# Zeroing the later keys with GpSimd instead of masking them with TensorE in the causal steps of two attention stages

## The chip, the cores and the metric

The kernel is one program on one core of a Trainium2 chip. The metric is the device time of the whole program in microseconds (us). Five engines work side by side, each through its own list of instructions in order, and they wait for each other on semaphores: PE is TensorE (PEld is its weight load), DVE is VectorE, ACT is ScalarE, POOL is GpSimd, SP is SyncE, which issues most DMAs.

## The reference

A decoder of four layers is computed for eight batches of 256 tokens of width 256. The change lies in two stages of layer 1, in which every batch has a causal softmax over its own 256 tokens with 16 heads of 16:

```python
# L1_attn, first half of the block (then LayerNorm, feed-forward, LayerNorm)
mask = (tq[:, :, None] >= tk[:, None, :]) & (tk[:, None, :] >= 0)
sim = jnp.where(mask[None], jnp.einsum('bnwd,bnkd->bnwk', qw, bk), -1000000000.0)
out = jnp.einsum('bnwk,bnkd->bnwd', jax.nn.softmax(sim, axis=-1), bv)

# L1_xattn, first of its two attentions (the second looks at 77 context rows, no mask)
scores = jnp.where(jnp.tril(...), q @ k * scale, finfo.min)
out = softmax(scores) @ v
```

Windows are 128 wide and each sees itself and the one before it, so for 256 tokens this is plain causal attention.

## The kernel before

Both stages are pipelined over steps p. In L1_attn there is one step for each batch (p = 0 to 7) and two more to drain. In L1_xattn there are sixteen: causal steps (called a) and context steps (b), in the order a0 a1 a2 b0 a3 b1 ... a7 b5 b6 b7. In step p the order of instructions of each engine is written out by hand; in it `now` is the batch of this step, `last` and `older` the two before, `soon` the next. Nothing is reordered later: an engine that waits stops everything behind the wait.

The attention of a causal batch goes like this.

- `pair_scores_tensor`, rounds 0 to 2: scores with queries in the partitions, 4 banks of PSUM (2048 columns). The later keys are masked by four matmuls of an identity with a mask of large negative numbers (`hide_later`, line 517). `pair_tops_vector` (line 569) takes each query's maximum, one VectorE reduction a round, and the next round reuses the banks, so TensorE and VectorE take turns here.
- `split_tops_vector` (lines 578 to 584) splits the maxima into three bf16 parts, `turn_tops_tensor` (592) transposes them, `turn_tops_scalar` (599) copies them out as `mT`.
- Turned scores, rounds 0 to 2, with keys in the partitions: `turned_first_tensor` and `turned_scores_tensor`. In each round four `hide_later` matmuls write the mask `keyC` to the banks, `turned_products` (line 621) adds the scores, and `turned_maxima` (line 630) subtracts the maxima. `turned_probs_scalar` (line 675) takes the exponential of 2048 columns into SBUF (`prob1` for round 0, `prob` for rounds 1 and 2) and raises `prob`; the next round may then overwrite the banks.
- `pair_outputs_tensor` c = 0 and 1 (lines 689 and 694) multiplies the probabilities of heads 8c to 8c+7 with the values; `pair_raw_scalar` (702) copies the results; `pair_back_tensor` (711) and `mean_vector` (721, 723) turn and divide them.

The tail of an L1_attn step on TensorE is, before: `turned_scores` 1; `own_v` of `soon` (line 416); `turned_scores` 2; outputs c = 0 of `now`; a wait for `kv` of `soon`, which VectorE raises in `own_v_vector` (line 796) and which frees PSUM bank 3; the queries of `soon` into bank 3; the second feed-forward product of `older`. The next step begins with scores 0 of the next batch, outputs c = 1 of this one, and the transposes of `older`. VectorE in the same step: three reductions, the split, `own_k_vector` (759), `mean_vector` of `last`, in steps 3 to 6 the second LayerNorm of batch p-3 (`outer_norm_vector`: statistics 2048 and 2052, a run of ten short dependent instructions at 2054 and 277 to 281, then 2057 and 2061), `own_v_vector` (796), the first LayerNorm of `last` (`inner_norm_vector`, from line 2087 on), `turned_z_vector` (830), `outer_sum_vector` (2096).

The tail of a causal L1_xattn step on TensorE: `turned_scores` 2, in some steps a product of the fp8 stage, outputs c = 0 of `now`; then the next step with its scores 0 (which wait for the last exponential) and outputs c = 1.

GpSimd does one bias addition for each batch in L1_xattn (line 864), and in L1_attn that and `x1b` (line 2266).

Of the kernel before, what the change touches and what calls it, by code (L numbers as in the profile page):

```python
# [18 lines left out]
ALU = mybir.AluOpType  # L19
# [3 lines left out]
P = 128  # L23
B, SEQ, D = 8, 256, 256
# [72 lines left out]
def places(fields):  # L97

    at, out = 0, {}
    for name, n in fields:  # L100
# [3 lines left out]

COMMON = ("done", "dve_step", "z", "zT_ps", "zT", "qkv_ps", "q", "kv", "s_ps", "s_sb", "prob", "probT_ps", "probT_a",
          "probT_v", "o_ps", "raw", "back_ps", "o", "oT_ps", "oT", "out_ps", "ctx")


# [70 lines left out]
def cut(ap, **sizes):  # L181
    (name, n), = sizes.items()
    return ap.rearrange(f"p ({name} f) -> p {name} f", **{name: n})
# [80 lines left out]
def mask_of(k, name):  # L264
    at, n = k.maskpos[name]
    return k.masks[:, at:at + n]
# [213 lines left out]
def narrow_signals(a):  # L480
    per = dict(kv_ps=1, kv=1, q_ps=1, q=1, s_ps=a.rounds, top=a.rounds, part=4, mT_ps=1, mT=1, t_ps=a.rounds,
               prob=a.rounds, o_ps=2, raw=2, back_ps=1, rec=1, o=1)
    if a.causal:
        per.update(z=1, zT_ps=1, zT=1, k_ps=1, k=1)
    return {a.p + name: n for name, n in per.items()}


# [28 lines left out]
def hide_later(k, out, mask):  # L516
    k.nc.tensor.matmul(out, k.identb[:, :], mask, start=True, stop=False, skip_group_check=True)  # L517
# [84 lines left out]
def turned_places(u, r):  # L602

    every, later, first, second, own = slice(0, SEQ), slice(P, SEQ), slice(0, P), slice(P, SEQ), slice(0, CTX)
    if not u.a.causal:
        return [(2 * r + ab, every, own, ab * SEQ) for ab in (0, 1)]
    if r == 0:
        return [(j, later, second, j * P) for j in range(4)]
    return [(2 * r - 2 + ab, every, first, ab * SEQ) for ab in (0, 1)]
# [26 lines left out]
def turned_first_tensor(k, pe, s, u, b, at=0):  # L636

    after(pe, s, u, "top", u.a.rounds)
    causal, places = u.a.causal, turned_places(u, 0)
    if causal:  # L640
        for i in range(4):
            hide_later(k, k.ps[:, HI + i, :], mask_of(k, "keyC"))
    else:
        turned_products(k, s, u, places[0], True, False)
    turn_tops_tensor(k, pe, s, u, b, at)
    for place in places if causal else places[1:]:
        turned_products(k, s, u, place, False, False)
    after(pe, s, u, "mT")
    for place in places:
        ins = turned_maxima(k, s, u, place, False, True)  # L650
    ins.then_inc(*s.sig.up(u.a.p + "t_ps"))


def turned_scores_tensor(k, pe, s, u, r):

    after(pe, s, u, "prob", r)
    if u.a.causal:
        for i in range(4):
            hide_later(k, cut(k.ps[:, HI + i, :], slot=4)[:, 0::2, :], mask_of(k, "keyC")[:, 0:2 * P])
    for place in turned_places(u, r):  # L660
        turned_maxima(k, s, u, place, not u.a.causal, False)
        ins = turned_products(k, s, u, place, False, True)
    ins.then_inc(*s.sig.up(u.a.p + "t_ps"))

# [14 lines left out]
def pair_outputs_tensor(k, pe, s, u, before, c):  # L679

    v, nk = s.v[u.at], u.a.nk
    after(pe, s, u, "prob", u.a.rounds - 1 + c)
    if u.a.causal:
        after(pe, s, u, "kv")
    after(pe, s, before, "o")
    for j in (2 * c, 2 * c + 1):
        at = j % 2 * SEQ
        for i in range(4):
            ins = k.nc.tensor.matmul(k.ps[PAD * i:PAD * i + u.a.vw, LO + c, at:at + SEQ], v[0:nk, 0, 4 * j + i, :],  # L689
                                     s.prob[0:nk, i, j * SEQ:(j + 1) * SEQ], start=True, stop=not u.a.causal,  # L690
                                     skip_group_check=True)
        if u.a.causal:
            for i in range(4):
                ins = k.nc.tensor.matmul(k.ps[PAD * i:PAD * i + VW, LO + c, at + P:at + SEQ], v[:, 1, 4 * j + i, :],
                                         s.prob1[:, i, j * P:(j + 1) * P], start=False, stop=True,
                                         skip_group_check=True)
    ins.then_inc(*s.sig.up(u.a.p + "o_ps"))


def pair_raw_scalar(k, act, s, u, c):  # L700
# [729 lines left out]

def L1_xattn_gpsimd(k, pool, s):
    enter(k, pool, s.sig)
    for n in range(B):
        bias_gpsimd(k, pool, s, n, "z", "bo2")


CHUNKS = 10
# [693 lines left out]
def L1_attn_tensor(k, pe, s):  # L2131
    pe.wait_ge(*s.behind.sig.at("f_out", 0, B - 1, 1))
    one = s.ahead
    own = one.steps[0]
    for p in range(B + 2):
        now, last, older, soon, _ = neighbours(s.steps, p)
        if now:
            pair_scores_tensor(k, pe, s, now, last, 0)
        if last:
            pair_outputs_tensor(k, pe, s, last, older, 1)  # L2140
        if older:
            after(pe, s, older, "x1")
            if p >= 3:
                after(pe, s, s.steps[p - 3], "sum")
            turn_tensor(k, s.x1[older.n % 2], k.ps[:, 2, :]).then_inc(*s.sig.up("x1T_ps"))
        if now:
            pair_scores_tensor(k, pe, s, now, last, 1)
        if soon:
            turned_z_tensor(k, pe, s, soon, 3)
        if p == B:  # L2150
            turned_z_tensor(k, pe, one, own, HI)
        if older:
            ff_up_tensor(k, pe, s, older, 0, 2)
        if p == B + 1:
            own_v_tensor(k, pe, one, own, HI + 3)
        if now:
            pair_scores_tensor(k, pe, s, now, last, 2)
        if last:
            pair_back_tensor(k, pe, s, last)
        if soon:  # L2160
            own_k_tensor(k, pe, s, soon, 3)
        if now:
            if older:
                after(pe, s, older, "f", 1)
            turned_first_tensor(k, pe, s, now, 2)
        if p == B:
            pe.wait_ge(*k.loaded["L1_xattn"])
            own_k_tensor(k, pe, one, own, HI + 1)
        if older:
            ff_up_tensor(k, pe, s, older, 1, 2)  # L2170
        if p == B:
            query_tensor(k, one, own, one.zT, HI + 2)
        if now:
            turned_scores_tensor(k, pe, s, now, 1)
        if soon:
            own_v_tensor(k, pe, s, soon, 3)
        if now:
            turned_scores_tensor(k, pe, s, now, 2)
            pair_outputs_tensor(k, pe, s, now, last, 0)
        if soon:  # L2180
            after(pe, s, soon, "kv")
            query_tensor(k, s, soon, s.zT, 3)
        if older:
            after(pe, s, older, "f", 2)
            token_out_tensor(k, s, s.f, w_of(k, s.stage, "ff2", FF // P), 2, FF // P).then_inc(*s.sig.up("out_ps"))


def L1_attn_scalar(k, act, s):
    one = s.ahead
    own = one.steps[0]  # L2190
    for p in range(B + 2):
        now, last, older, soon, _ = neighbours(s.steps, p)
        if last:
            pair_raw_scalar(k, act, s, last, 1)
        if older:
            after(act, s, older, "x1T_ps")
            k.nc.scalar.activation(flat(s.x1T), k.ps[:, 2, :], ACT.Copy).then_inc(*s.sig.up("x1T"))
        if soon:
            turned_z_scalar(k, act, s, soon, 3)
        if p == B:  # L2200
            turned_z_scalar(k, act, one, own, HI)
        if older:
            ff_up_scalar(k, act, s, older, 0, 2)
        if now:
            turn_tops_scalar(k, act, s, now, 2)
            turned_probs_scalar(k, act, s, now, 0)
        if older:
            ff_up_scalar(k, act, s, older, 1, 2)
        if p == B:
            query_scalar(k, act, one, own, HI + 2)  # L2210
        if now:
            turned_probs_scalar(k, act, s, now, 1)
            turned_probs_scalar(k, act, s, now, 2)
            pair_raw_scalar(k, act, s, now, 0)
        if soon:
            query_scalar(k, act, s, soon, 3)


def L1_attn_vector(k, dve, s):
# [36 lines left out]
            outer_sum_vector(k, dve, s, older, 2)  # L2256


def L1_attn_gpsimd(k, pool, s):
    enter(k, pool, s.sig)  # L2260
    for u in s.steps:
        bias_gpsimd(k, pool, s, u.n, "z", "ln2_b")
        pool.wait_ge(*s.sig.at("x1", 0, u.n, 1))
        if u.n >= 2:
            pool.wait_ge(*s.sig.at("sum", 0, u.n - 2, 1))
        k.nc.gpsimd.tensor_tensor(s.x1b[u.n % 2], s.x1[u.n % 2],
                                  spread_of(k, s.stage, "ff2b").unsqueeze(1).broadcast_to([P, 2, D]), ALU.add)\
            .then_inc(*s.sig.up("x1b"))

# [3040 lines left out]
```

## Time and profile before

| | us |
|---|---|
| three timed runs | 3136.51, 3142.32, 3145.74 |
| their median | 3142.32 |
| the profiled execution, from first to last instruction | 3146.4 |
| TensorE busy in it | 2939.7 (93%) |
| VectorE busy | 1864.8 (59%) |
| ScalarE busy | 1253.5 (40%) |
| GpSimd busy | 435.9 (14%) |

A row of the timeline has the start of a run of equal instructions in us from the start of the span, its length, engine, line, operation, operands with shapes, and how many there are. In brackets stands how long the engine had been idle and which engine and line ended the wait. The first mask matmul of the changed stages starts at 1136.6 and the last at 1681.1; L1_attn fills about 1136 to 1400, L1_xattn 1400 to 1700.

### The profile page before, as it was taken

How to read it: one execution, taken by the hardware profiler on the slowest of the kernel's cores; microseconds unless marked ns; L12 is line 12 of the kernel's file. 1: busy time of each engine (PE TensorE's matmuls, PEld its weight loads, DVE VectorE, ACT ScalarE, POOL GpSimd, SP SyncE). 2: the span in 40 equal slices, each digit the busy share in tenths (PEclk: the TensorE clock that was granted, in tenths of full speed). 3: DMA queues.
4: the chain of work that ended last, by engine and by line, in shares of the span. 5: the costliest groups of instructions: out<-in, count | busy, mean ns of one | idle time of the engine just before them, and what ended most of it. 6: DMA issues, size and time to landing. Idle time of an engine off the chain costs nothing.

```text
span 3146.4 us, 52294 instructions
## 1 busy us (share of the span) xinstructions
PE 2939.7 (93%) x20677; PEld 1953.5 (62%) x20677; DVE 1864.8 (59%) x6449; ACT 1253.5 (40%) x1946; POOL 435.9 (14%) x458
## 2 busy tenths in 40 slices
PE   7999999998989889988998999899999999998998
PEld 4666666875555556655665566566666766766653
DVE  5534433599999636775777898574244344434455
ACT  2222221335656433323444678544323333323443
POOL 0010010114433221000000356300000000000000
PEclk9999999988999999999999899899999999998999
DMA  3000000010000100000000111100000000000000
GB/s 130 1 1 0 1 1 1 1 53 1 2 1 2 34 32 1 1 1 6 1 2 1 25 39 28 41 2 27 1 1 0 1 0 1 1 1 9 2 1 27
DMA packets 22028, 37.75 MB, mean 12 GB/s; under 512 B 2132, under 2 KB 19733, under 8 KB 20760
## 3 DMA queue, kind: packets, MB, share of 16 engines
q1 hardware_dynamic: 20968, 34.02, 3.2%
q8 instruction: 163, 2.67, 0.3%
q14 instruction: 81, 0.66, 0.1%
q10 hardware_dynamic: 816, 0.39, 0.1%
HBM read 26.81 MB, written 2.10 MB: 9 GB/s over the span
## 4 chain that ended last, share of the span: by engine, by line
PE 76%; DVE 17%; ACT 4%; issue 2%; DMA 0%; ACTq 0%; DVEq 0%; SPq 0%; POOL 0%; POOLq 0%
PE ps L416 44%; DVE arena L569 3%; PE ps L621 2%; PE ps L689 2%; PE ps L3098 2%; PE ps L3117 2%; ACT arena L675 2%; PE ps L1633 2%; PE ps L517 2%; PE ps L2353 2%; PE ps L2399 2%; DVE arena L1967 2%; PE ps L730 2%; PE ps L711 1%; PE ps L2971 1%
## 5 line engine op out<-in xcount | busy, mean ns | idle before, releaser
L416 PE MATMUL ps<-weights,arena 128*128 128x256 f32 (+4 forms) x2480 | 694.3, 429 | 41.3 <-DVE arena L1848 22.5
L416 PEld LDWEIGHTS ps<-weights,arena 128*128 128x128 f32 (+1 forms) x2480 | 459.5, 195 | 210.8 <-issue 92.9
L416 PE MATMUL ps<-arena,weights 128*128 128x256 f32 (+4 forms) x1726 | 558.9, 472 | 14.0 <-DMA weights<-in_w_L_attn 6.1
L416 PEld LDWEIGHTS ps<-arena,weights 128*128 128x128 f32 (+1 forms) x1726 | 315.1, 191 | 217.0 <-issue 156.5
L416 PE MATMUL ps<-arena 128*128 128x256 f32 (+4 forms) x1618 | 425.8, 416 | 6.8 <-ACT arena L4816 1.5
L416 PEld LDWEIGHTS ps<-arena 128*128 128x128 f32 (+2 forms) x1618 | 297.9, 188 | 115.4 <-issue 74.3
L569 DVE TENSOR_REDUCE arena<-ps 128x16 f32<-128x1232 f32 (+2 forms) x96 | 179.1, 1866 | 151.0 <-PE ps L547 51.8
L675 ACT ACTIVATE arena<-ps 77x2048 f32<-77x2048 f32 (+1 forms) x112 | 210.0, 1875 | 123.9 <-PE ps L621 61.8
L1967 DVE MATCH_REPLACE8 arena<-arena 128x77 f32<-128x77 f32 x1024 | 214.7, 228 | 0.0
L864 POOL TENSOR_TENSOR x<-x,weights 128x512 f32<-128x512 f32 x32 | 43.8, 1370 | 1194.9 <-DVE arena L830 1147.2
L2366 ACT ACTIVATE arena<-ps 128x1536 f32<-128x1536 f32 x128 | 185.5, 1451 | 51.4 <-PE ps L2355 44.6
L2384 POOL TENSOR_SCALAR_AFFINE_SELECT arena<-arena 128x512 f32<-128x512 f32 x128 | 147.5, 1154 | 217.6 <-ACT arena L2366 217.1
L1960 DVE MAX8 arena<-arena 128x8 f32<-128x77 f32 x1024 | 154.1, 229 | 0.2 <-DVE rstd L281 0.2
L4199 DVE COPY arena<-ps 128x1024 f32<-128x1024 f32 x16 | 19.6, 1225 | 203.8 <-PE ps L416 203.8
L4061 ACT ACTIVATE arena<-ps 128x512 f32<-128x512 f32 x128 | 76.4, 597 | 119.7 <-PE ps L416 119.6
L621 PE MATMUL ps<-arena 32*77 32x256 f32 (+2 forms) x1792 | 120.5, 368 | 1.1 <-DVE arena L569 1.1
L2375 DVE TENSOR_TENSOR arena<-arena 128x512 f32<-128x512 f32 x128 | 91.7, 717 | 44.3 <-ACT arena L2366 43.4
L730 PE MATMUL ps<-ident,arena 128*128 128x128 f32 x544 | 90.3, 290 | 29.2 <-POOL arena L2002 7.7
L517 PE MATMUL ps<-masks,identb 128*128 128x256 bf16 (+1 forms) x384 | 72.9, 313 | 39.5 <-DVE arena L569 26.1
L689 PE MATMUL ps<-arena 77*17 77x256 f32 (+2 forms) x1536 | 108.4, 390 | 0.2 <-ACT arena L675 0.2
L702 ACT ACTIVATE arena<-ps 128x512 f32<-128x512 f32 x96 | 57.1, 595 | 128.9 <-PE ps L689 68.4
L2353 PE MATMUL ps<-arena 32*128 32x256 bf16 x512 | 103.4, 278 | 3.0 <-DMA arena<-arena 2.6
(430 smaller groups left out, 4437.6 us busy)
## 6 DMA issues: line engine op xcount, KB each, us to landing
arena<-arena SPq DMA_DIRECT2D x156, 32.0 KB
weights<-in_w_L_ffn SPq DMA_DIRECT2D x1, 3848.0 KB, 11.5
weights<-in_w_L_attn SPq DMA_DIRECT2D x1, 3840.0 KB, 15.1
weights<-in_w_L_xattn SPq DMA_DIRECT2D x3, 1024.0 KB, 6.3
weights<-in_w_L_ffn SPq DMA_DIRECT2D x1, 3072.0 KB, 10.2
x<-in_x SPq DMA_DIRECT2D x2, 1024.0 KB
weights<-in_w_L_xattn SPq DMA_DIRECT2D x1, 2048.0 KB, 7.4
out<-x SPq DMA_DIRECT2D x8, 256.0 KB, 2.2
```

What stands on the lines that cost most here:

```text
L416: ins = k.nc.tensor.matmul(out, lhsT, rhs, start=start and i == 0, stop=i == n - 1)
L517: k.nc.tensor.matmul(out, k.identb[:, :], mask, start=True, stop=False, skip_group_check=True)
L569: k.nc.vector.tensor_reduce(out, src, AX, ALU.max).then_inc(*s.sig.up(u.a.p + "top"))
L621: ins = k.nc.tensor.matmul(k.ps[0:u.a.nk, HI + i, out], kT[group(i)], qT[group(i)], start=fresh, stop=stop, skip_group_check=True)
L675: k.nc.scalar.activation(out, k.ps[0:u.a.nk, HI:HI + 4, :], ACT.Exp, scale=u.a.scale)\
L689: ins = k.nc.tensor.matmul(k.ps[PAD * i:PAD * i + u.a.vw, LO + c, at:at + SEQ], v[0:nk, 0, 4 * j + i, :], s.prob[0:nk, i, j * SEQ:(j + 1) ...
L730: ins = k.nc.tensor.transpose(out[:, (2 * c + t) * P:(2 * c + t + 1) * P], src[:, t, c * P:(c + 1) * P], k.ident[:, :])
L1960: ins = k.nc.vector.max(tops, left)
L1967: ins = k.nc.vector.match_replace(left, tops, left, -BIG)
L2353: mm(k.ps[:, base + u // 2, u % 2 * SEQ:(u % 2 + 1) * SEQ], kk[:, 0:P], q, start=True, stop=True, skip_group_check=True)
L2366: k.nc.scalar.activation(s.prob[at % PROBS], k.ps[:, base:base + 3, :].rearrange("p b f -> p (b f)"), ACT.Exp, scale=NH1 ** -0.5).then_inc ...
L2384: k.nc.gpsimd.affine_select(diag, diag, [[0, 4], [1, P]], ALU.is_ge, 0.0, base=0, channel_multiplier=-1)\
```

## The change

The `hide_later` matmuls of all three rounds of turned scores are gone. `hide_second_gpsimd` and `hide_first_gpsimd` are new: for each c, once the exponentials are in SBUF, GpSimd selects in place over the diagonal blocks and writes 0.0 where the key is later than the query, eight instructions of 128 x 512 a batch. They raise a new semaphore `hidden` four times a batch, and outputs c of a causal batch wait for its count 2c + 2. In round 0 two places' products (before: the masks) go ahead of the transposes of the maxima. In L1_attn outputs c = 0 and their copy by ScalarE move behind the queries of `soon` (and on TensorE behind the feed-forward product). GpSimd's list in L1_attn becomes: bias of u, the eight selects of u, then `x1b` of u-1; in L1_xattn bias of n, then its eight selects.

```diff
 def turned_first_tensor(k, pe, s, u, b, at=0):
-    causal, places = u.a.causal, turned_places(u, 0)
-    if causal:
-        for i in range(4):
-            hide_later(k, k.ps[:, HI + i, :], mask_of(k, "keyC"))
-    else:
-        turned_products(k, s, u, places[0], True, False)
+    places = turned_places(u, 0)
+    ahead = 2 if u.a.causal else 1
+    for n, place in enumerate(places[:ahead]):
+        turned_products(k, s, u, place, n == 0, False)
     turn_tops_tensor(k, pe, s, u, b, at)
-    for place in places if causal else places[1:]:
+    for place in places[ahead:]:
         turned_products(k, s, u, place, False, False)
...
 def turned_scores_tensor(k, pe, s, u, r):
     after(pe, s, u, "prob", r)
-    if u.a.causal:
-        for i in range(4):
-            hide_later(k, cut(k.ps[:, HI + i, :], slot=4)[:, 0::2, :], mask_of(k, "keyC")[:, 0:2 * P])
     for place in turned_places(u, r):
-        turned_maxima(k, s, u, place, not u.a.causal, False)
+        turned_maxima(k, s, u, place, True, False)
...
 def pair_outputs_tensor(k, pe, s, u, before, c):
     if u.a.causal:
         after(pe, s, u, "kv")
+        after(pe, s, u, "hidden", 2 * c + 2)
...
+def hide_second_gpsimd(k, pool, s, u, c):
+    after(pool, s, u, "prob", 1)
+    for j in (2 * c, 2 * c + 1):
+        prob = s.prob1[:, :, j * P:(j + 1) * P]
+        ins = k.nc.gpsimd.affine_select(prob, prob, [[0, 4], [1, P]], ALU.is_ge, 0.0, base=0, channel_multiplier=-1)
+    ins.then_inc(*s.sig.up(u.a.p + "hidden"))
+
+def hide_first_gpsimd(k, pool, s, u, c):
+    after(pool, s, u, "prob", 2 + c)
+    for j in (2 * c, 2 * c + 1):
+        prob = s.prob[:, :, j * SEQ:j * SEQ + P]
+        ins = k.nc.gpsimd.affine_select(prob, prob, [[0, 4], [1, P]], ALU.is_ge, 0.0, base=0, channel_multiplier=-1)
+    ins.then_inc(*s.sig.up(u.a.p + "hidden"))
...
 def L1_attn_tensor(k, pe, s):
             turned_scores_tensor(k, pe, s, now, 2)
-            pair_outputs_tensor(k, pe, s, now, last, 0)
         if soon:
             after(pe, s, soon, "kv")
             query_tensor(k, s, soon, s.zT, 3)
         if older:
             after(pe, s, older, "f", 2)
             token_out_tensor(...)
+        if now:
+            pair_outputs_tensor(k, pe, s, now, last, 0)
...
 def L1_attn_scalar(k, act, s):
-            pair_raw_scalar(k, act, s, now, 0)
         if soon:
             query_scalar(k, act, s, soon, 3)
+        if now:
+            pair_raw_scalar(k, act, s, now, 0)
```

## Rows read from the trace of the kernel before

**Rows 1.** The page: shares of the chain that ended last, and the mask matmuls.

```profile
PE 76%; DVE 17%; ACT 4%; issue 2%; DMA 0%; ACTq 0%; DVEq 0%; SPq 0%; POOL 0%; POOLq 0%
...
L517 PE MATMUL ps<-masks,identb 128*128 128x256 bf16 (+1 forms) x384 | 72.9, 313 | 39.5 <-DVE arena L569 26.1
```

**Rows 2.** Timeline of TensorE, tail of L1_attn step 3 (start, length in us).

```profile
1239.96 0.40 PE L630 MATMUL ps<-arena,pick 32*128 32x128 bf16 x16
...
1242.34 0.61 PE L517 MATMUL ps<-masks,identb 128*128 128x256 bf16 x4
...
1242.88 0.29 PE L630 MATMUL ps<-arena,pick 32*128 32x256 bf16 x4
...
1244.08 1.99 PE L416 MATMUL ps<-weights,arena 128*128 128x256 f32 x8
...
1247.89 0.63 PE L689 MATMUL ps<-arena 128*17 128x256 f32 x8
...
1249.32 1.99 PE L416 MATMUL ps<-arena,weights 128*128 128x256 f32 x8
...
1251.15 3.62 PE L416 MATMUL ps<-weights,arena 128*128 128x256 f32 x16
...
1254.60 1.03 PE L517 MATMUL ps<-masks,identb 128*128 128x512 bf16 x4
```

**Rows 3.** Timeline of ScalarE, same step: copy of the maxima, exponentials 0 and 1.

```profile
1239.07 0.38 ACT L599 ACTIVATE arena<-ps 128x256 bf16<-128x256 bf16 x1 [4.67 <-PE ps L592]
...
1240.40 1.88 ACT L675 ACTIVATE arena<-ps 128x2048 f32<-128x2048 f32 x1 [0.95 <-PE ps L630]
...
1244.22 1.88 ACT L675 ACTIVATE arena<-ps 128x2048 f32<-128x2048 f32 x1 [1.06 <-PE ps L621]
```

**Rows 4.** Timeline of VectorE, same step, up to the next step's first reduction.

```profile
1242.51 0.17 DVE L2054 TENSOR_SCALAR arena<-arena 128x2 f32<-128x2 f32 x1
...
1244.68 0.88 DVE L2057 SCALAR_TENSOR_TENSOR arena<-arena,weights 128x256 f32<-128x256 f32 x2
...
1247.29 0.67 DVE L796 TENSOR_TENSOR arena<-ps,weights 128x512 f32<-128x512 f32 x1
...
1256.77 2.29 DVE L569 TENSOR_REDUCE arena<-ps 128x16 f32<-128x2048 f32 x1 [0.72 <-PE ps L547]
```

**Rows 5.** Line 2384: GpSimd's selects in L2_attn, ns min/median/max.

```profile
L2384 POOL TENSOR_SCALAR_AFFINE_SELECT arena<-arena x128: 630/1151/4427, 1748.2 to 2000.5; 128x512 f32<-128x512 f32 x128
```

**Rows 6.** Timeline, GpSimd and VectorE side by side in L1_attn.

```profile
1253.77 1.68 DVE L830 TENSOR_SCALAR arena<-x,norm,rstd 128x256 f32<-128x256 f32 x2
...
1253.94 1.37 POOL L2266 TENSOR_TENSOR arena<-arena,weights 128x512 f32<-128x512 f32 x1 [28.10 <-DVE arena L2061]
```

**Rows 7.** Timeline of VectorE, the same two instructions without GpSimd.

```profile
1513.92 0.73 DVE L830 TENSOR_SCALAR arena<-x,norm,rstd 128x256 f32<-128x256 f32 x2
```

**Rows 8.** Timeline of TensorE, L1_attn step 0: waits before round 1 and step 1.

```profile
1153.89 0.80 PE L517 MATMUL ps<-masks,identb 128*128 128x256 bf16 x4 [1.97 <-ACT arena L675]
...
1165.12 1.04 PE L517 MATMUL ps<-masks,identb 128*128 128x512 bf16 x4 [0.93 <-ACT arena L810]
```

**Rows 9.** Windows: length, busy time of each engine, TensorE's granted clock, DMA.

```profile
1154.00:1159.00 5.00, 5.00 (x36) 3.21 (x35) 0.00 (x0) 1.88 (x1) 0.00 (x0) 0.66 0.01 3
...
1200.00:1358.00 158.00, 152.84 (x1520) 103.39 (x1524) 117.85 (x276) 55.19 (x74) 13.07 (x10) 1.00 0.01 1
```

**Rows 10.** Timeline of TensorE, end of L1_xattn step a3 and start of b1.

```profile
1514.05 0.66 PE L730 MATMUL ps<-ident,arena 128*128 128x128 f32 x4
...
1520.08 0.61 PE L517 MATMUL ps<-masks,identb 128*128 128x256 bf16 x4
...
1521.82 0.63 PE L689 MATMUL ps<-arena 128*17 128x256 f32 x8
...
1523.99 0.81 PE L539 MATMUL ps<-arena 32*128 32x154 f32 x16 [0.67 <-ACT arena L675]
...
1524.72 0.63 PE L689 MATMUL ps<-arena 128*17 128x256 f32 x8
```

More of the change, by code:

```diff
@@ L103, in places @@
     return out, at
-COMMON = ("done", "dve_step", "z", "zT_ps", "zT", "qkv_ps", "q", "kv", "s_ps", "s_sb", "prob", "probT_ps", "probT_a",
+COMMON = ("done", "dve_step", "z", "zT_ps", "zT", "qkv_ps", "q", "kv", "s_ps", "prob", "hidden", "probT_ps", "probT_a",
           "probT_v", "o_ps", "raw", "back_ps", "o", "oT_ps", "oT", "out_ps", "ctx")
@@ L483, in narrow_signals @@
     if a.causal:
-        per.update(z=1, zT_ps=1, zT=1, k_ps=1, k=1)
+        per.update(z=1, zT_ps=1, zT=1, k_ps=1, k=1, hidden=4)
     return {a.p + name: n for name, n in per.items()}
@@ L1432, in L1_xattn_gpsimd @@
     enter(k, pool, s.sig)
-    for n in range(B):
-        bias_gpsimd(k, pool, s, n, "z", "bo2")
+    for u in s.steps:
+        if u.a.causal:
+            bias_gpsimd(k, pool, s, u.n, "z", "bo2")
+            for c in (0, 1):
+                hide_second_gpsimd(k, pool, s, u, c)
+                hide_first_gpsimd(k, pool, s, u, c)
 CHUNKS = 10
@@ L2256, in L1_attn_vector, with inner_bias_gpsimd @@
             outer_sum_vector(k, dve, s, older, 2)
+def inner_bias_gpsimd(k, pool, s, u):
+    after(pool, s, u, "x1")
+    if u.n >= 2:
+        pool.wait_ge(*s.sig.at("sum", 0, u.n - 2, 1))
+    k.nc.gpsimd.tensor_tensor(s.x1b[u.n % 2], s.x1[u.n % 2],
+                              spread_of(k, s.stage, "ff2b").unsqueeze(1).broadcast_to([P, 2, D]), ALU.add)\
+        .then_inc(*s.sig.up("x1b"))
 def L1_attn_gpsimd(k, pool, s):
@@ L2262, in L1_attn_gpsimd @@
         bias_gpsimd(k, pool, s, u.n, "z", "ln2_b")
[L2263 to L2268, printed above, removed]
+        for c in (0, 1):
+            hide_second_gpsimd(k, pool, s, u, c)
+            hide_first_gpsimd(k, pool, s, u, c)
+        if u.n:
+            inner_bias_gpsimd(k, pool, s, s.steps[u.n - 1])
+    inner_bias_gpsimd(k, pool, s, s.steps[B - 1])
 GROUPS = NH1 // 4
```

## The prediction

> **What bounds the kernel now.** I read the page first: the chain that ended last runs 76% of the span through TensorE, and the mask matmuls that this change halves (192 of 384 go) are 72.9 us of busy time [rows 1]. So the naive hope is some 36 us. Then the windows: in the steady part of L1_attn TensorE is busy 152.8 of 158.0 us, but VectorE is busy 117.9, and that is with forced pauses [rows 9]. So I read one step engine by engine. The reader is to see two things. First, TensorE's tail of step 3 has no gap: outputs 0 start at 1247.89, the queries of the next batch at 1249.32, the feed-forward product at 1251.15, the next step's mask at 1254.60 [rows 2]. Second, VectorE runs from its split to the next step almost without a gap too: it waits only 0.72 us for the next scores before the reduction at 1256.77 [rows 4]. The period is 29.59 us. TensorE can gain only as far as VectorE lets it.
>
> **The change part by part, L1_attn, steps 3 to 6.** All times are on the clock of step 3, whose third reduction, and so the split, does not move.
>
> *Masks removed.* Round 0: its maxima (line 630) started at 1239.96; they also need the copy of the maxima, which ends at 1239.07 + 0.38 = 1239.45 [rows 2, 3]. The masks and their order go, so they start at about 1239.50: 0.46 gained. Two places' products now fill the wait for the split and cost nothing. Rounds 1 and 2 lose one mask each: 1242.88 - 1242.34 = 0.54 [rows 2]. Exponential 0 starts 0.46 earlier, at 1239.95, exponential 1 by 1.0, at about 1243.25 [rows 3]. The turned scores are done 1.5 us earlier: at 1246.4 instead of 1247.89.
>
> *Outputs 0 moved.* What stands next on TensorE is now the wait for `kv` of the next batch. VectorE raises it at 1247.29 + 0.67 = 1247.96 [rows 4]. Before, outputs 0 (1249.32 - 1247.89 = 1.43 us) covered that wait; now nothing does. From `kv` on TensorE has the same work as before: queries 1.83, product 3.45, outputs 1.43, together 6.71 us [rows 2]. With an undisturbed VectorE the next step starts at 1248.0 + 6.7 = 1254.75, against 1254.60 before. All 1.5 us are gone, whatever the masks saved. The wait of outputs 0 for `hidden` is covered by that work: exponential 1 ends at 1245.1, two selects are far earlier than 1253. ScalarE's queries come before the raw copy now, which is worth nothing here because TensorE does not wait for them.
>
> *Selects added.* GpSimd gets 8 a step. The nearest row is the same operation on 128 x 512: 630 ns at least, 1151 median, 4427 at most [rows 5]. The low end is its time when VectorE leaves it alone; 5.0 to 9.2 us a step. GpSimd itself has room. The question is what VectorE loses. The two bias operations show it: VectorE's two instructions of line 830 take 1.68 us with GpSimd's line 2266 beside them and 0.73 without [rows 6, 7]. So one GpSimd instruction can hold VectorE for its own length. The Trainium skill says why, on the page "SBUF — State Buffer", section "Who interferes with whom": VectorE instructions with two SBUF inputs, or in a two-port mode, and GpSimd's instructions that read SBUF exclude each other for a whole instruction. This trace agrees (1.68 against 0.73 us); by that rule reductions and additions out of PSUM are spared, and by a reading of the masks alone the cost would be nothing.
>
> Exponential 0 ends at 1241.83. Selects 1 and 2 run to about 1243.3, beside the short dependent instructions that begin at 1242.51 [rows 4]; one of them waits some 0.6. Exponential 1 ends at 1245.1, when VectorE is about to do lines 2057 and 2061 (1244.68 before, now 1245.3), pairs with two SBUF inputs. Each of the pairs waits for one select: 2 x 0.6. That makes 1.85 us ahead of `own_v_vector` (between 0 and five selects, 3.1). `kv` comes at 1249.8, and the next step starts at 1249.85 + 6.71 = 1256.6: 2.0 us later than before. The last selects fall on line 796, which reads PSUM, and on `inner_norm_vector`, whose end is not the bound: VectorE's own loop has 0.72 us spare and gets about 0.5 more of delay, which stays under the 2.0.
>
> *TensorE's clock.* TensorE now idles from 1246.4 to 1249.8, 3.4 us. In step 0 it had idled 1.97 us, and the 5 us behind show a granted clock of 0.66 [rows 8, 9], that is some 3.4 us at 1.2 GHz of 2.4. Half of 3.4, 1.7 us of work, is then lost; none if the stretch falls into waits. I take 1.5. So a step of this kind costs 2.0 + 1.5 = 3.5 us (between 0.15 and 5), and there are four (3 to 6): +14.
>
> **L1_attn, the other steps.** Step 0: the next step's first mask had waited 0.93 us for the queries' copy [rows 8], which now stands ahead of the raw copy, and the masks' 1.5 us go; VectorE has time. I take -1.9. Step 1: VectorE has no gap before step 2, its chain starts 1.3 earlier and is hit by selects for about 1.8: +0.5. Step 2 has no second LayerNorm, so `kv` is early: -0.8. Step 7 has neither queries nor `kv`, but VectorE runs two LayerNorms in a row with every dependent instruction open to the eight selects, and step 8 waits for their end: +3 (0 to 4). Together +0.8, and L1_attn +14.8.
>
> **L1_xattn.** Step a3: the gain of round 0 dies, because the transposes at 1514.05 start when `mean_vector` of the last batch is done, and VectorE does not move [rows 10]. Rounds 1 and 2 give 0.54 each. Exponential 1 ended just before the mask at 1520.08 [rows 10], now 0.53 earlier, at 1519.50. Two selects later, 1520.85, outputs 0 may start; TensorE is there at 1520.75. Before it was 1521.82: 0.9 gained. The next scores waited 0.67 us for exponential 2 and started at 1523.99 [rows 10]; that exponential is 1.07 earlier, so they start at 1522.9. Outputs 1, before at 1524.72, now need the last select, which follows exponential 2 (1522.8) by 1.3: 1524.15. Gain 0.5. Steps with fp8 work on VectorE give GpSimd less room; over six such steps I take 0.3 each, -1.8. Steps a0 and a1 are followed by a longer causal scores block, which hides `hidden`: -1.3 each. L1_xattn -4.4.
>
> **Sum.** +14.8 - 4.4 = +10.4 us. The profiled execution had 3146.4 us as its span, 4.1 (0.13%) above the median of the timed runs; I put the difference on the median: 3142.3 + 10.4 = 3153.
>
> **The rivals.**
> 1. *VectorE isn't hit before `kv`*, because selects slip behind its instructions. The median of 1151 ns, far over 630 [rows 5], says that it is often GpSimd which waits; line 830 says the contrary [rows 6]. Then steps 3 to 6 cost 0.15 each, an idle of 1.5 us leaves the clock alone, steps 0, 1, 2, 7 give about -4.5, L1_xattn -4.4: -8, 3134.
> 2. *The masks' time comes out in full*, as the mask rows by themselves say: 1.5 us in each of 16 steps, -24 at most, about 3120. It needs `kv` 1.5 us earlier, against it stands row 1247.29 [rows 4].
> 3. *GpSimd becomes the bound in L1_xattn*, the other side by a longer way: at 1.15 us a select, the c = 1 selects end 1519.50 + 6 x 1.15 = 1526.4 plus small gaps, so outputs 1 start at 1526.5 instead of 1524.72, +1.8 in six steps, +11; and VectorE loses up to 3.1 in L1_attn's steps (+4.6 each, with the clock, +18). Together about +28, 3170. It decides as soon as a select takes more than (1524.72 - 1519.50) / 6 = 0.87 us. For it speaks the median; against, that VectorE in a3 is mostly reading PSUM or idle.
>
> **How the numbers follow.** The forecast has 0.45 (own range 3146 to 3163), rival 1 0.25, rival 2 0.13, rival 3 0.17. The range 3126 to 3172 holds all but most of rival 2 and tails. A measurement tells about 0.3%, 9.4 us, from no change: faster is below 3132.9, slower above 3151.7. Faster: rival 2 and 0.10 of rival 1, 0.23. Slower: rival 3 and 0.26 of the forecast, 0.43. The same: 0.34.
>
> **What would show it.** In step 3's like of the changed kernel: turned scores 2 end 1.5 us earlier after the third reduction; line 416 for the queries idles 2 to 4 us for VectorE line 796; lines 277 to 281, 2057 or 2061 show one instruction of 0.5 us or more beside a select; the granted clock in steps 3 to 6 is below 1.00, where it was 1.00 [rows 9]; the period is 33 instead of 29.59 us. In L1_xattn outputs 1 start without a wait of over 0.7 us for GpSimd. The prediction is wrong if selects run 0.63 us and line 796 does not move (rival 1), or if the queries find `kv` done (rival 2).

## The result, and the profile after

| | before | changed |
|---|---|---|
| median of the first series (4 runs each) | 3143.81 us | 3164.68 us |
| ratio, 95% interval | | 1.0055 [1.0037, 1.0073] |
| repeated beside other kernels (34 and 12 runs) | 3145.26 us | 3155.86 us, 1.0040 [1.0028, 1.0052] |
| span of the profiled execution | 3146.4 us | 3150.1 us, repeated 3153.3 us |

The change makes the kernel slower, by 17 us by the ratio of the first series and by 13 us by that of the repeated one (the medians of the table lie 21 and 11 us apart). The forecast was 3153 us, +10.4, with a range up to 3172.

Where the time went can be read from the end of each step's last reduction (line 569), which both kernels have. The table gives the periods between these ends.

| from the last reduction of ... to that of ... | before | changed | repeated | forecast | found |
|---|---|---|---|---|---|
| L1_attn step 0 to 1 | 29.12 | 26.59 | 26.61 | -1.9 | -2.5 |
| step 1 to 2 | 29.67 | 28.46 | 28.47 | +0.5 | -1.2 |
| step 2 to 3 | 29.59 | 28.12 | 28.12 | -0.8 | -1.5 |
| steps 3 to 4, 4 to 5, 5 to 6, 6 to 7 | 4 x 29.59 | 34.18, 31.69, 33.38, 33.38 | 31.70, 33.38, 33.38, 34.43 | +14 | +14.3 |
| step 7 to L1_xattn a0 | 60.50 | 64.16 | 63.92 | +3 | +3.7 |
| a0 to b7 | 308.94 | 306.41 | 306.55 | -4.4 | -2.5 |
| together | | | | +10.4 | +10.2 |

Outside this part the two profiles differ too, by some us either way, in stages whose code is the same. The last reduction of step 0 itself ends at 1149.28 before and at 1146.14 in the changed kernel. From b7's last reduction to the next stage's first one at line 569 the profiles of this study range from 284.1 to 291.0 us (before 291.0, changed 288.1, repeated 290.9). The time of the whole program is therefore the rougher measure here, and the step the finer one.

The changed kernel's timeline of TensorE from step 4, to be put beside [rows 2]. Its clock zero is the third reduction's end, 1263.49 here and 1237.67 before, so before's times are to be raised by 25.82.

```profile
1265.27 0.40 PE L630 MATMUL ps<-arena,pick 32*128 32x128 bf16 x16
...
1267.66 0.29 PE L630 MATMUL ps<-arena,pick 32*128 32x256 bf16 x4
...
1271.60 0.61 PE L621 MATMUL ps<-arena 32*128 32x256 f32 x8
1275.71 1.99 PE L416 MATMUL ps<-arena,weights 128*128 128x256 f32 x8 [3.51 <-DVE arena L810]
1277.55 3.62 PE L416 MATMUL ps<-weights,arena 128*128 128x256 f32 x16
1281.09 0.63 PE L685 MATMUL ps<-arena 128*17 128x256 f32 x8
```

The reader is to see two things. The turned scores end at about 1272.2, which is 1.5 us earlier than before's 1247.89 + 25.82 = 1273.71: the masks' time is really saved. And then TensorE stands for 3.51 us, released by line 810 of VectorE (before: line 796, `own_v_vector`), and starts the queries at 1275.71, 0.57 later than before (1249.32 + 25.82 = 1275.14), with the outputs still to come at 1281.09.

VectorE before had a second pair of instructions behind line 2057 of [rows 4]:

```profile
1245.59 0.88 DVE L2061 SCALAR_TENSOR_TENSOR x<-arena,x 128x256 f32<-128x256 f32 x2
```

VectorE of the changed kernel's step 4, and GpSimd (lines 701 and 710 are the selects of round 0 and of rounds 1 and 2):

```profile
1268.33 0.59 DVE L2072 TENSOR_SCALAR arena<-arena 128x2 f32<-128x2 f32 x1
1268.96 0.17 DVE L277 TENSOR_SCALAR arena<-arena 128x2 int32<-128x2 int32 x1
...
1270.92 1.71 DVE L2075 SCALAR_TENSOR_TENSOR arena<-arena,weights 128x256 f32<-128x256 f32 x2
1272.67 1.50 DVE L2079 SCALAR_TENSOR_TENSOR x<-arena,x 128x256 f32<-128x256 f32 x2
1274.32 0.75 DVE L860 BATCH_NORM_STATS2 stats<-x 128x6 f32<-128x256 f32 x2
1274.99 0.67 DVE L810 TENSOR_TENSOR arena<-ps,weights 128x512 f32<-128x512 f32 x1
...
1284.70 2.29 DVE L569 TENSOR_REDUCE arena<-ps 128x16 f32<-128x2048 f32 x1 [0.95 <-PE ps L547]
```

```profile
1267.68 1.23 POOL L701 TENSOR_SCALAR_AFFINE_SELECT arena<-arena 128x512 f32<-128x512 f32 x2 [17.57 <-ACT arena L670]
1270.95 1.41 POOL L710 TENSOR_SCALAR_AFFINE_SELECT arena<-arena 128x512 f32<-128x512 f32 x2 [2.05 <-ACT arena L670]
1272.31 1.58 POOL L701 TENSOR_SCALAR_AFFINE_SELECT arena<-arena 128x512 f32<-128x512 f32 x2
1274.22 1.22 POOL L710 TENSOR_SCALAR_AFFINE_SELECT arena<-arena 128x512 f32<-128x512 f32 x2 [0.33 <-ACT arena L670]
```

An instruction over 2 elements (line 2072) takes 0.59 us instead of 0.17, beside the second select. The pairs 2075 and 2079 take 3.25 us from the first start to the last end where they took 1.8 (1244.68 to 1246.47). The statistics of line 860 and line 810, which reads PSUM, have the last two selects beside them from 1274.22 on and keep their 0.75 and 0.67 us. So `own_v_vector` ends 12.17 us behind the third reduction, against 10.29 before: 1.88 us later.

TensorE's granted clock, in windows over most of each of steps 3 to 6 of the changed kernel, where before had 1.00 throughout [rows 9] (length, busy times, clock, DMA):

```profile
1230.00:1263.00 33.00, 28.70 (x274) 19.70 (x268) 24.48 (x56) 10.89 (x14) 8.05 (x10) 0.90 0.01 1
...
1264.00:1295.00 31.00, 26.70 (x276) 18.35 (x277) 24.89 (x56) 10.89 (x14) 8.05 (x10) 1.00 0.00 1
1296.00:1328.00 32.00, 27.69 (x268) 18.88 (x264) 24.22 (x55) 10.88 (x14) 8.05 (x10) 0.95 0.01 2
1329.00:1362.00 33.00, 26.91 (x265) 17.97 (x266) 23.62 (x56) 10.29 (x13) 7.91 (x10) 0.95 0.00 1
```

Step 4 kept 2.4 GHz (1.00) and has the shortest period, 31.69. Steps 5 and 6, each with one stretch at 1.2 GHz that brings the mean to 0.95, have 33.38, 1.69 more, with the same instructions. Step 3, at 0.90, spent twice as long at 1.2 GHz and has 34.18, 2.5 more.

### The profile page after: what moved, and what is told of

Read it like the earlier page. It is cut to its first block, busy times and chain, and to the rows that moved or that the text cites. A ratio compares the mean times of both kernels' runs of the same rounds, so it can differ in the third digit from the quotient of the medians.

```text
span 3150.1 us, 52042 instructions
## 1 busy us (share of the span) xinstructions
PE 2915.0 (93%) x20461; PEld 1942.9 (62%) x20485; DVE 1875.1 (60%) x6449; ACT 1255.4 (40%) x1946; POOL 519.0 (16%) x586
## 3 DMA queue, kind: packets, MB, share of 16 engines
q8 instruction: 162, 2.65, 0.3%
## 4 chain that ended last, share of the span: by engine, by line
PE 73%; DVE 20%; ACT 4%; issue 3%; POOL 0%; DMA 0%; DVEq 0%; SPq 0%; ACTq 0%; POOLq 0%
PE ps L416 44%; DVE arena L569 3%; PE ps L685 2%; PE ps L3128 2%; PE ps L3147 2%; PE ps L1651 2%; PE ps L621 2%; PE ps L2429 2%; PE ps L2383 2%; PE ps L744 2%; DVE arena L1985 2%; ACT arena L670 1%; PE ps L3001 1%; PE ps L554 1%; DVE arena L1978 1%
## 5 line engine op out<-in xcount | busy, mean ns | idle before, releaser
L3268 POOL TENSOR_TENSOR x<-x,arena 128x1024 f32<-128x1024 f32 (+1 forms) x17 | 34.0, 1997 | 463.5 <-DVE arena L3243 463.5
L744 PEld LDWEIGHTS ps<-ident,arena 128*128 128x128 f32 x544 | 62.6, 146 | 74.0 <-issue 30.6
## 6 DMA issues: line engine op xcount, KB each, us to landing
weights<-in_w_L_ffn SPq DMA_DIRECT2D x1, 3072.0 KB, 10.2
```

The source lines that it names most:

```text
L744: ins = k.nc.tensor.transpose(out[:, (2 * c + t) * P:(2 * c + t + 1) * P], src[:, t, c * P:(c + 1) * P], k.ident[:, :])
```

## The experiments

All were timed in five rounds beside the kernel before. "Region" is the change against before from the last reduction of step 0 of L1_attn to that of a0, and from there to that of b7, in the one profile of each.

| kernel | ratio to before, 95% | periods of steps 3 to 6 | region |
|---|---|---|---|
| changed, repeated | 1.0040 [1.0028, 1.0052] | 31.70, 33.38, 33.38, 34.43 | +12.7, -2.4 |
| no_selects | 0.9960 [0.9947, 0.9974] | 29.82, 29.83, 29.82, 29.83 | -7.7, -5.4 |
| move_only | 0.9986 [0.9975, 0.9996] | 29.82, 3 x 29.83 | -0.6, -1.4 |
| outputs_back | 1.0020 [1.0008, 1.0032] | 3 x 30.66, 30.17 | +5.7, -2.0 |
| ff_first | 1.0018 [1.0004, 1.0032] | 32.02, 33.39, 31.97, 29.06 | +9.6, -0.3 |
| late_selects | 1.0033 [1.0021, 1.0045] | 30.92, 30.92, 30.93, 29.83 | +12.3, -0.4 |
| xattn_only | 0.9999 [0.9989, 1.0010] | 4 x 29.59 | -0.6, -0.5 |
| early_ff | 0.9990 [0.9980, 1.0000] | 4 x 29.70 | -0.9, -2.7 |
| first_cut | 1.0018 [1.0003, 1.0032] | 32.58, 30.89, 30.90, 30.90 | +5.1, -2.9 |
| more_selects | 1.0062 [1.0047, 1.0077] | 33.38, 34.22, 31.70, 33.38 | +19.2, -0.6 |
| first_step | 1.0002 [0.9991, 1.0013] | 4 x 29.82 | -3.5, -1.3 |

**The changed kernel again.**

> The changed kernel once more, as the measure for its neighbours. My theory (GpSimd's selects hold VectorE up by about 1.9 us ahead of own_v_vector in L1_attn steps 3 to 6, and with outputs 0 moved away TensorE waits for kv in the open, over 3 us, and often runs at 1.2 GHz behind it): +10 to +20 us against before; periods of steps 3 to 6 between 31.7 us (clock held) and 34.2. If the extra time of three of its four runs came from elsewhere, the periods would stay as in the first profile (34.18, 31.69, 33.38, 33.38) and another stage would be longer.

Met: +12.6 us by the ratio, and nearly the same set of periods in another order. Which step meets the low clock changes; the lengths hardly do (the longest is 34.43 instead of 34.18).

**No selects.** The zeroing is left out altogether.

```diff
-        after(pe, s, u, "hidden", 2 * c + 2)
...
             for c in (0, 1):
-                hide_second_gpsimd(k, pool, s, u, c)
-                hide_first_gpsimd(k, pool, s, u, c)
+                pass
+                pass
```

> Leaves out the zeroing of later keys altogether (no masks in the turned scores, no selects, no wait for them); the order of outputs 0 is the changed kernel's. My theory: VectorE lines 2072 to 2079 are back at their length, kv comes 1.9 us earlier, TensorE idles about 1.5 us instead of 3.4 before the queries, periods of steps 3 to 6 are 29.6 to 29.9; against before -8 to -18 us. Rival, the moved outputs alone are the cost: these periods stay above 31. Rival, the masks' time comes out in full once nothing else is added: periods of 28.1 and -24 us.

Met: -12.6 us, so the selects cost 0.8% of the time, 25 us, while the removed masks and the moved outputs together gave only half of that. The rows of VectorE and TensorE in step 4:

```profile
1262.03 0.17 DVE L2071 TENSOR_SCALAR arena<-arena 128x2 f32<-128x2 f32 x1
...
1264.20 0.88 DVE L2074 SCALAR_TENSOR_TENSOR arena<-arena,weights 128x256 f32<-128x256 f32 x2
1265.12 0.88 DVE L2078 SCALAR_TENSOR_TENSOR x<-arena,x 128x256 f32<-128x256 f32 x2
```

```profile
1267.55 1.99 PE L416 MATMUL ps<-arena,weights 128*128 128x256 f32 x8 [1.64 <-DVE arena L809]
```

VectorE is back at its lengths and still TensorE waits 1.64 us for `kv`: in these steps the removed masks give nothing (29.82 against 29.59). What is gained comes from steps 0 to 2 (-8.1 us), from step 7 to a0 (-0.6) and from L1_xattn (-5.4). That rules out rival 2 of the prediction.

**The move alone.** The two orders of the change on the kernel before (ScalarE's copy moves too, which the cut doesn't show).

```diff
             turned_scores_tensor(k, pe, s, now, 2)
-            pair_outputs_tensor(k, pe, s, now, last, 0)
...
+        if now:
+            pair_outputs_tensor(k, pe, s, now, last, 0)
```

> The kernel before, with outputs 0 and their copy moved to the step's end as in the change; masks stay on TensorE, no selects. My theory: the turned scores end at 1247.9 on the clock of step 3 and kv comes at 1248.0, so the move costs 0.15 us in steps 3 to 6 and saves up to 0.9 us after steps 0 and 1 where the next scores waited for the queries' copy: -2 to +1 us, the same. Rival, the move is the cost: +6 us or more.

Steps 3 to 6 cost 0.23 more each, as expected in kind, steps 0 and 1 are 1.6 and 1.0 shorter. The time missed my -2 to +1 on the good side: -4.4 us by the ratio, though its interval reaches to -1.3 and the profile's region has only -2.0. The move by itself isn't the cost.

**Outputs 0 back ahead of the queries**, and ScalarE's copy of them too.

```diff
             turned_scores_tensor(k, pe, s, now, 2)
+            pair_outputs_tensor(k, pe, s, now, last, 0)
...
-        if now:
-            pair_outputs_tensor(k, pe, s, now, last, 0)
```

> The changed kernel with outputs 0 and their copy back ahead of the queries in L1_attn. My theory: they wait 0.1 to 0.2 us for the selects and then cover 1.4 us of the wait for kv, so TensorE's idle ahead of the queries falls from 3.4 to about 1.8 us and the low clock is rarer; the bound then is VectorE, periods of steps 3 to 6 about 30.7; against the changed kernel -7 to -11 us, against before +1 to +8. Rival, TensorE's wait for GpSimd's selects is what costs: outputs 0 now wait at once for them, the kernel is as slow as the changed one or slower.

Nearly met: half of the loss is gone (1.0020), -6.3 us against the changed kernel where I had put -7 to -11, and +6.3 against before. TensorE in step 4 waits twice, briefly for GpSimd and then for VectorE:

```profile
1273.88 0.63 PE L685 MATMUL ps<-arena 128*17 128x256 f32 x8 [0.40 <-POOL arena L710]
1276.98 1.99 PE L416 MATMUL ps<-arena,weights 128*128 128x256 f32 x8 [1.61 <-DVE arena L810]
```

The wait for GpSimd's selects is 0.40 us and the kernel is faster, so that wait is not what costs (the rival). The period is 30.66 in three steps, without a stretch of low clock, and VectorE's first reduction follows its last sum without a gap: VectorE is the bound at 30.7.

```profile
1284.95 2.28 DVE L569 TENSOR_REDUCE arena<-ps 128x16 f32<-128x2048 f32 x1
```

**The feed-forward product ahead of the queries.**

```diff
+        if older:
+            token_out_tensor(...)
         if soon:
             after(pe, s, soon, "kv")
             query_tensor(k, s, soon, s.zT, 3)
-        if older:
-            token_out_tensor(...)
```

> The changed kernel with the second feed-forward product of older ahead of the wait for kv and the queries in L1_attn. My theory: that product (3.45 us) covers TensorE's idle of 3.4 us whole, the clock stays at 2.4 GHz, and what is left is VectorE's own loop with the selects' delay in it: in step 4 of the changed kernel it had 0.95 us to spare at a period of 31.69, so 30.7. Against the changed kernel -8 to -12 us, against before 0 to +5. If VectorE isn't held up in total but only ahead of kv, the period falls to 29.0 and the time 4 to 6 us below before.

The wait for `kv` is covered, and the ratio is just outside the ranges (-7 us against the changed kernel where I had put -8 to -12, +5.7 against before where I had put 0 to +5). But the periods of steps 3 to 5 were not 30.7: TensorE's idle moved to the waits at the reductions, and TensorE met the low clock there, just where VectorE waits for its scores. Step 6, which has less VectorE work and met no low clock, took 29.06. VectorE's waits ahead of the two later reductions are 1.80 us each before; here, in the step that took 33.39:

```profile
1287.88 2.28 DVE L569 TENSOR_REDUCE arena<-ps 128x16 f32<-128x2048 f32 x1
1293.34 2.29 DVE L569 TENSOR_REDUCE arena<-ps 128x8 f32<-128x2048 f32 x1 [3.18 <-PE ps L554]
1298.80 2.29 DVE L569 TENSOR_REDUCE arena<-ps 128x8 f32<-128x2048 f32 x1 [3.17 <-PE ps L554]
```

**Late selects.** All eight of an L1_attn step behind the last exponential.

```diff
-    after(pool, s, u, "prob", 1)
+    after(pool, s, u, "prob", 3 if s.stage == "L1_attn" else 1)
...
-    after(pool, s, u, "prob", 2 + c)
+    after(pool, s, u, "prob", 3 if s.stage == "L1_attn" else 2 + c)
```

> The changed kernel with all eight selects of L1_attn behind the last exponential (some 10.5 us behind the third reduction), as two runs of work, so that none can fall ahead of own_v_vector. My theory: lines 2072 to 2079 of outer_norm_vector are back at their length, kv comes 1.9 us earlier, TensorE idles 1.6 us and not 3.5 ahead of the queries; but the selects now fall on inner_norm_vector's dependent instructions and delay VectorE's end instead: periods of steps 3 to 6 of 30 to 32 us, against the changed kernel -4 to -12 us. Rival, the selects cost by their number on GpSimd and not by where they fall: periods as in the changed kernel, 31.7 to 34.2.

In steps 3 to 6 it went as expected: 30.92, the pairs at their old length, the wait for `kv` 1.63 us; the selects now lie beside `inner_norm_vector`:

```profile
1276.91 0.88 DVE L2075 SCALAR_TENSOR_TENSOR arena<-arena,weights 128x256 f32<-128x256 f32 x2
1277.83 0.88 DVE L2079 SCALAR_TENSOR_TENSOR x<-arena,x 128x256 f32<-128x256 f32 x2
...
1282.12 0.36 DVE L2072 TENSOR_SCALAR arena<-arena 128x2 f32<-128x2 f32 x1
...
1286.42 0.88 DVE L2075 SCALAR_TENSOR_TENSOR arena<-arena,weights 128x256 f32<-128x256 f32 x2
```

From line 2072 to line 2075 it takes 4.3 us where 2.17 are usual. The total missed (only -2 us against the changed kernel): steps 0 to 2, which I had left out, now have periods of 30.5, 30.8 and 31.0 instead of 26.6, 28.5 and 28.1. In steps 0 and 1 outputs 0 now wait 2.65 and 2.75 us for the late selects (line 685, released by line 710).

**The selects of rounds 1 and 2 cut to 4 columns.** Most later keys of these rounds are not zeroed.

```diff
+    n = 4 if s.stage == "L1_attn" else P
-        prob = s.prob[:, :, j * SEQ:j * SEQ + P]
+        prob = s.prob[:, :, j * SEQ:j * SEQ + n]
```

> The changed kernel, but in L1_attn the selects of rounds 1 and 2 (line 710) cover 4 columns of each block and not 128, so most later keys of those rounds are not zeroed; round 0's selects are whole. My theory: only the selects of round 0 hold VectorE up by their length, 0.4 us in line 2072, and the four of line 710 by about 0.1 each at most; kv comes 1.2 to 1.4 us earlier than in the changed kernel, TensorE idles 2.0 to 2.3 us ahead of the queries, periods of steps 3 to 6 are 30.2 to 30.6 (a stretch at 1.2 GHz adds up to 1.7); against the changed kernel -8 to -14 us, against before 0 to +5. Rival, an instruction of GpSimd costs VectorE the same whatever its length: periods as in the changed kernel.

A select over 128 x 16 takes 0.23 us in most cases (0.21 at least), and VectorE's first pair is nearly free of it; `own_v_vector` ends 11.4 us behind the reduction, halfway between 10.3 and 12.2. The size of my split was off: 0.8 of the 1.9 us are rounds 1 and 2, because the c = 1 selects of round 0 (1273.85) still fall on the second pair. Shorter selects in the same places cost less, so the rival, a cost that doesn't depend on their length, is out. The periods are 30.9 and TensorE's wait 2.70 us, over my 30.2 to 30.6 and 2.0 to 2.3, and the time missed too: -6.9 us against the changed kernel instead of -8 to -14, +5.7 against before instead of 0 to +5.

```profile
1270.07 1.23 POOL L701 TENSOR_SCALAR_AFFINE_SELECT arena<-arena 128x512 f32<-128x512 f32 x2 [16.77 <-ACT arena L670]
1273.34 0.55 POOL L711 TENSOR_SCALAR_AFFINE_SELECT arena<-arena 128x16 f32<-128x16 f32 x2 [2.04 <-ACT arena L670]
1273.85 1.64 POOL L701 TENSOR_SCALAR_AFFINE_SELECT arena<-arena 128x512 f32<-128x512 f32 x2
```

**Four more selects a batch**, which change nothing in the data.

```diff
+        if s.stage == "L1_attn":
+            ins = k.nc.gpsimd.affine_select(rest, rest, [[0, 4], [1, P]], ALU.is_ge, 0.0, base=P, channel_multiplier=-1)
```

> The changed kernel with four more selects a batch in L1_attn, on the right half of each block of rounds 1 and 2, where the predicate holds everywhere and nothing changes. My theory: VectorE's lines 2075 and 2079 already met a select each, so they stay at 3.25 us and kv does not move by more than 0.5 us; the added selects fall on inner_norm_vector and lengthen VectorE's loop by 1 to 2.5 us, from 30.7 to 32 or 33, so that it is level with TensorE's: periods of steps 3 to 6 between 32 and 35, against the changed kernel +1 to +6 us. Rival, the cost goes by the number of selects wherever they fall: 3.5 us a step for eight, so 5.2 for twelve, +7 us or more.

Met for the pairs and for `kv`: the pairs (lines 2077 and 2081 there) take the same 3.25 us, TensorE waits the same 3.50, and the periods are of the same three kinds, 31.7, 33.4, 34.2. So in steps 3 to 6 half as many selects again cost nothing more. VectorE's own loop grew by only 0.3 us and not by 1 to 2.5: in the step of 31.70 it still waits 0.64 us for its scores (the changed kernel 0.95), so TensorE stays the bound. The kernel is +19.5 us by the ratio, 7 more than the changed one beside its neighbours; in the profile they lie in steps 1 and 2 (30.79 and 29.10 instead of 28.46 and 28.12) and from step 7 to a0 (66.54 instead of 64.16). That is over my +1 to +6, and by its size alone the rival's +7 us is met; the place speaks against it.

```profile
1274.63 1.71 DVE L2077 SCALAR_TENSOR_TENSOR arena<-arena,weights 128x256 f32<-128x256 f32 x2
1276.37 1.51 DVE L2081 SCALAR_TENSOR_TENSOR x<-arena,x 128x256 f32<-128x256 f32 x2
...
1279.28 0.81 DVE L2107 TENSOR_TENSOR arena<-arena 128x512 f32<-128x512 f32 x1
```

**Looking for a better version.** Three kernels keep the masks where VectorE is full. In all, a step can be marked to keep its masks:

```diff
-def step(a, n, at):
+def step(a, n, at, masked=False):
...
+    if u.masked:
+        for i in range(4):
+            hide_later(k, k.ps[:, HI + i, :], mask_of(k, "keyC"))
```

> The change in L1_xattn alone; L1_attn has its masks on TensorE and its old order. My theory: from a0 to b7 the changed kernel gained 2.5 us in its profile, so -1 to -5 us against before. Rival, GpSimd becomes the bound there: slower than before by 5 us or more.

> The parts that pay put together: the selects in L1_xattn and in steps 0 to 2 of L1_attn, the masks on TensorE in steps 3 to 7 of L1_attn, outputs 0 at the step's end, the feed-forward product ahead of the queries. My theory: steps 0 to 2 give -5 us as in the changed kernel, steps 3 to 6 run at 29.6, step 7 as before, L1_xattn -2.5: -5 to -10 us against before, and the same or a little slower than the kernel that left the zeroing out (-12.6).

> The moved outputs 0 in all of L1_attn, the selects only in its step 0 (VectorE has no LayerNorm there) and in L1_xattn, masks on TensorE in steps 1 to 7. My theory: the move by itself gave -4.4 us (-0.5 in its profile from step 0 to b7), step 0's selects -1, L1_xattn -2.5: -4 to -8 us against before, periods of steps 3 to 6 29.83 as with the move alone. Rival, what the small runs gained was only the luck of TensorE's clock: 0 to -2 us.

None is told from before by more than 0.1%. L1_xattn alone, 0.9999, missed its -1 to -5. early_ff, -3.1 us, missed its -5 to -10; first_step missed its -4 to -8 and came out at 1.0002, although its profile gained 4.8 us in the region. The steps are as long as was expected (0.3 us less from a2 to b0 and from a3 to b1, 29.7 or 29.8 in steps 3 to 6), but the starts of the stages lose as much again in some profiles (a1 to a2: 26.40 before, 27.45 in xattn_only); that this is TensorE's low clock alone is not shown. Whether these versions are better by a few us stays open. Of all kernels with the whole computation, the move alone has the best ratio, 0.9986.

## Why the prediction was right

The forecast's sign, its range and its mechanism held, and in steps 3 to 6, where it expected the loss, each term came out within 0.3 us. That the whole came to +10.2 in the profile against +10.4 is luck: steps 0 to 2 gained 3.0 us more than forecast, while L1_xattn gained 1.9 less and steps 3 to 7 lost 1.0 more. Point by point:

- *The masks' 1.5 us.* Right to 0.1: the turned scores end 1.5 us earlier. They are worth nothing in steps 3 to 6, as forecast: no_selects has 29.82, and 29.74 was worked out for an undisturbed VectorE (29.59 + 0.15).
- *VectorE held up by 1.85 us ahead of `own_v_vector`.* Measured 1.88, in the places named: 0.4 in the short instructions and 1.45 in the two pairs. So rival 1 is out. That undisturbed length and that place are shown by no_selects, late_selects and more_selects, not only argued.
- *TensorE's idle of 3.4 us.* 3.51. *The clock, 1.5 us a step.* 1.69 when one stretch was met, 2.5 to 2.7 in the two longest periods, 0 in one step of four in each profile, 1.5 in the mean. With the 2.1 us of the step at 2.4 GHz (31.69 - 29.59) the four steps came to +3.6 each against +3.5.
- *Step 7, +3.* +3.7. Without selects this part takes 59.92 us, 4.2 less than in the changed kernel. Of the 4.2, 3.2 are VectorE's sum, for which TensorE's transposes wait: they start 21.55 us behind step 7's last reduction (1361.90) with the selects and 18.38 behind it (1346.70) without. The rest goes with TensorE's clock: from there on (1383.45 to 1393.0) it is granted 0.84, without selects (1365.08 to 1375.0) 1.00, and the same transposes take 1.94 us and not 1.06.

```profile
1383.45 1.94 PE L744 MATMUL ps<-ident,arena 128*128 128x128 f32 x8 [4.77 <-DVE arena L2114]
```

```profile
1365.08 1.06 PE L743 MATMUL ps<-ident,arena 128*128 128x128 f32 x8 [3.30 <-DVE arena L2113]
```

- *Steps 0 to 2, -2.2.* -5.2: mis-sized. In step 0 the 0.6 us beyond the forecast are before's: it met a stretch at 1.2 GHz at the step's end (granted clock 0.80 from 1170.0 to 1178.4), where its last reduction waited 2.42 us instead of 1.81. Step 1 was forecast at +0.5 and came out at -1.2, and both of its terms were off. VectorE's chain, which starts when TensorE's `own_v` product is done, begins 11.09 us behind step 1's last reduction before and 8.99 in the changed kernel, 2.1 us earlier and not 1.3. From there to the next last reduction it takes 18.58 before, 19.47 with the selects and 18.60 without: the selects cost 0.9 us and not 1.8. The whole step is 2.45 us shorter without selects (26.01), but 1.6 of that is the clock: the changed kernel's `own_v` product takes 3.58 us at a granted clock of 0.90 (1172.7 to 1190.0), that of no_selects 1.99 at 1.00. Step 2 was forecast at -0.8 and gave the masks' full 1.5: it has 28.12 in the changed kernel and in no_selects alike, because VectorE has time there. TensorE and VectorE of step 1, changed (last reduction of step 1 at 1172.73) and then no_selects (at 1173.24):

```profile
1178.11 3.58 PE L416 MATMUL ps<-weights,arena 128*128 128x256 f32 x8
...
1181.72 0.69 DVE L810 TENSOR_TENSOR arena<-ps,weights 128x512 f32<-128x512 f32 x1 [5.24 <-PE ps L416]
```

```profile
1178.62 1.99 PE L416 MATMUL ps<-weights,arena 128*128 128x256 f32 x8
...
1180.65 0.69 DVE L809 TENSOR_TENSOR arena<-ps,weights 128x512 f32<-128x512 f32 x1 [3.66 <-PE ps L416]
```

- *L1_xattn, -4.4.* -2.5. The mechanism in a3 is as told: outputs 0 wait 0.22 us for GpSimd, outputs 1 0.60 us.

```profile
1529.20 0.63 PE L685 MATMUL ps<-arena 128*17 128x256 f32 x8 [0.22 <-POOL arena L710]
...
1531.07 0.81 PE L539 MATMUL ps<-arena 32*128 32x154 f32 x16 [0.38 <-ACT arena L670]
1532.47 0.63 PE L685 MATMUL ps<-arena 128*17 128x256 f32 x8 [0.60 <-POOL arena L710]
```

  The passages from a causal step to its context step gained 0.3 for a2 and a3, 0.05 for a4 to a6 and 0.5 for a7, -1.3 for the six; a4 to a7 have the fp8 work. Without selects (no_selects) they gained 1.0, 0.4 and 1.0, so here too the selects take half or more of what the masks gave. a0 and a1 gave -1.2 instead of -2.6, and that isn't the selects: no_selects has the same two periods, 28.20 and 25.71. Both kernels have a granted clock of 0.88 and 0.93 there, before 0.94 and 1.00; that the missing 1.4 us are this clock is likely and not shown.
- *Rival 3, a select of 1.15 us.* Ruled out by the row of the selects (ns min/median/max), against the 870 ns at which it would have decided: the low end of [rows 5] is the one that applied.

```profile
L710 POOL TENSOR_SCALAR_AFFINE_SELECT arena<-arena x64: 630/637/1142, 1154.0 to 1692.3; 128x512 f32<-128x512 f32 x64
```

The steps explain +10.2 us. The timed runs say +12.6 and, in the first series, +17 (down to +12 by its interval), where the forecast of 3153 is 12 us below the median. The rest is not placed: both profiled executions of the changed kernel were at or below the median of their series.

## What to carry to other kernels

Work moved to an idle engine is priced by whom it holds up, not by that engine's free time: GpSimd was busy 8 of 31 us here and cost more than the masks on the full TensorE. Before removing work from a full engine, look for the wait that its work covers and ask which engine sets that wait's end; if it is one without slack, the time saved turns into idle at once. And where TensorE is full, keep some independent product to stand in front of such a wait, but count where the idle goes next.

## What the runs showed of the hardware

- A GpSimd select over 128 x 512 took 637 ns at the median here (64 of line 710, 630 to 1142 ns), also when VectorE waited for it, as line 2072 did. In L2_attn the same operation had 1151 [rows 5]; there, for 84 of the 128, VectorE's line 2375, which has two SBUF inputs, had started ahead of it, 35 ns at the median.
- Independent VectorE instructions with two SBUF inputs and selects took turns one by one: four instructions and the selects between them took 3.25 us instead of 1.8, and three of the four selects 0.81 to 0.82 us instead of 0.64. This agrees with the exclusive lock that the Trainium skill describes ("SBUF — State Buffer", "Who interferes with whom").
- After an idle of 3.5 us TensorE stayed at 2.4 GHz in step 4 and fell to 1.2 GHz in steps 3, 5 and 6, so the length of one idle did not decide it. In ff_first it fell without any idle over 1.5 us: in the step of 33.39 it had waited 1.29 and then 1.48 us, and the granted clock from 1288.0 to 1301.1 is 0.74.
